# A selective scan on one core: every fourth state's output product moved from VectorE to GpSimd

## The chip, the core and the metric

The kernel runs on one core of a Trainium2 chip, as one launch that computes eight layers of a network on 3125 nodes. The metric is device time in microseconds. The change lies in one stage of the third layer, the selective scan.

## The reference, cut to what matters

The scan is the middle of `_mamba`. It runs along the 3125 nodes (in a sorted order) for 256 channels, each with 16 states.

```python
# dt, xc, z: [3125, 256]; Bm, Cm: [3125, 16]
A = -jnp.exp(A_log)                                # [256, 16]
dA = jnp.exp(dt[:, :, None] * A)                   # decay of each channel and state
dBx = (dt * xc)[:, :, None] * Bm[:, None, :]       # what each node drives into the state
def step(h, t):
    dA_t, dBx_t, C_t = t
    h = dA_t * h + dBx_t
    return (h, h @ C_t)                            # sum over the 16 states of h * C
_, y = lax.scan(step, jnp.zeros((256, 16)), (dA, dBx, Cm))
y = y + xc * D_param
y = y * jax.nn.silu(z)
return y @ out_proj_w.T
```

So for each state there is a recurrence along the nodes, and its result is multiplied by that state's row of `Cm` and summed over the states.

## The kernel before

`selective_scan` holds the channels on partitions (two halves of 128) and the nodes along the free dimension. The nodes are cut into 7 cuts of up to 447 (`CUTS`; the last has 443). Steps run over cut by cut and, inside a cut, over the 16 states: 112 steps, n = 16 x cut + state. In one step both halves lie side by side, 894 columns.

For step n the engines do this:

- SP loads the state's two rows, of B and of C, from `k.bc_d` in HBM and broadcasts them over all 128 partitions into `rows`, buffer n mod 4 (L2879). Before it reuses a buffer it waits until the drive (`ins_done`) and ScalarE's copy (`c_done`) of step n-4 are done (L2876, L2877). At state 4 of a cut it also loads `xc` and `z` for that cut.
- GpSimd makes the drive: row of B times `u` into `dB`, which has 3 buffers (L2899). It waits for the loaded row and for the scan of step n-3. From the second cut on it adds the carry of the cut before to the first column (L2904). At states 11 and 15 it also scatters one or two finished tiles each of the cut before with indirect DMAs (`move`, L2891).
- ScalarE makes the decays `dA` in PSUM, 2 buffers (L2945, L2946), two steps ahead; reads the carry out of `hh` (L2978); and copies the row of C into `row_c`, a single buffer in PSUM (L2956), when the product before is done.
- VectorE runs the recurrence over the 894 columns as one instruction, `dA` and `dB` into `hh`, 2 buffers (L3005), and then the product `pr` = `row_c` x `hh`, 2 buffers (L3013). Its order is scan n+1, product n. After a cut it adds `xc` x `dp` and multiplies by `z` (`finish`, L3020 and L3023), between the second scan and the first product of the next cut.
- TensorE adds each `pr` into `ps_y` by a multiplication with the identity (L2931), and projects the finished tiles of the cut before at states 4 and 9.

The order of the work on each engine is written out by hand; semaphores tie the engines together. GpSimd cannot read `row_c`, which is in PSUM; `rows` is in SBUF.

Of the kernel before, what the change touches and what calls it, by code (L numbers as in the profile page):

```python
# [8 lines left out]
ALU = mybir.AluOpType  # L9
# [2826 lines left out]
def selective_scan(k, z, dt, u, a_log, d_param, w_out, table):  # L2836


    nc = k.nc
    SN, CH, R = STATES, 447, 4  # L2840
# [2 lines left out]
    PROJECT_AT, KEEP_AT, MOVE_AT = (4, 9), (6, 11), (11, 15)  # L2843
    done_by = [0] + [hi // P for _, hi in CUTS]
    pair_of = lambda c, e: [t for t in range(done_by[c], done_by[c + 1]) if (t - done_by[c]) // 2 == e]
    moved_before = lambda n: sum(len(pair_of(q // 2, q % 2)) for q in range(n) if q % 2 == n % 2)
    with stage(k) as s:
        al, A, dp = s.sb("al", [128, 2, SN]), s.sb("A", [128, 2, SN]), s.sb("dp", [128, 2])
# [4 lines left out]
        xc = s.sb("xc", [128, 2, 2, CH])  # L2853
        dA, row_c, ps_y, ps_p = s.ps("dA", [128, 2, 1024]), s.ps("row_c", [128, 512]), s.ps("ps_y", [128, 2, 512]), s.ps("ps_p", [P, 2, D])
        gated, p_mm, p_read, moved = s.sem("gated"), s.sem("p_mm"), s.sem("p_read"), [s.sem(f"moved{e}") for e in range(2)]
        loaded, raised, negated, exps, carried, mixed, ins_done, c_done, scanned, prods, y_mm, y_read = (
            s.sem(n) for n in ("loaded", "raised", "negated", "exps", "carried", "mixed", "ins", "c_done", "scanned", "prods", "y_mm", "y_read"))
        cut_off, faded = s.sem("cut_off"), s.sem("faded")
        row_in = [s.sem(f"row_in{b}") for b in range(R)]
        pair_in = [s.sem(f"pair_in{c}") for c in range(len(CUTS))]  # L2860
# [6 lines left out]
        with s.block() as block:  # L2867
            @block.sync
            def _(sp):
                sp.dma_start(al[:], a_log.rearrange("(c p) n -> p c n", p=128)).then_inc(loaded, 16)  # L2870
                with nc.allow_non_contiguous_dma(reason="one number a channel"):
                    sp.dma_start(dp[:], d_param.rearrange("(c p) -> p c", p=128)).then_inc(loaded, 16)
                sp.dma_start(w_sb[:], w_out.rearrange("(c p) f -> p c f", p=128)).then_inc(loaded, 16)
                for n in range(STEPS):
                    if n >= R:
                        sp.wait_ge(ins_done, n - R + 1)  # L2876
                        sp.wait_ge(c_done, n - R + 1)  # L2877
                    lo, hi = cut(n)
                    sp.dma_start(rows[:, n % R, :, 0:hi - lo], k.bc_d[:, n % SN, lo:hi].partition_broadcast(128)).then_inc(row_in[n % R], 16)  # L2879
                    if n % SN == R:  # L2880
                        if n // SN >= 2:
                            sp.wait_ge(gated, n // SN - 1)
                        sp.dma_start(xc[:, n // SN % 2, :, 0:hi - lo], k.xc_d[:, :, lo:hi].rearrange("c p n -> p c n")).then_inc(pair_in[n // SN], 16)
                        sp.dma_start(z[:, :, lo:hi], k.z_d[:, :, lo:hi].rearrange("c p n -> p c n")).then_inc(pair_in[n // SN], 16)

            @block.gpsimd
            def _(pool):
                def move(c, e):
                    pool.wait_ge(p_read, 2 * c + e + 1)
                    for i, t in enumerate(pair_of(c, e)):  # L2890
                        nc.gpsimd.indirect_dma_start(table, bass.IndirectOffsetOnAxis(k.order_i[:, t:t + 1], 0), kept[:, e, i, :], None).then_inc(moved[e], 16)  # L2891

                for n in range(STEPS):
                    lo, hi = cut(n)
                    pool.wait_ge(row_in[n % R], 16 * (n // R + 1))
                    if n >= 3:
                        pool.wait_ge(scanned, n - 2)
                    into = halves(dB[:, n % 3, :], hi - lo)
                    ins = nc.gpsimd.tensor_tensor(into, both(rows[:, n % R, 0, 0:hi - lo], hi - lo), u[:, :, lo:hi], ALU.mult)  # L2899
                    if n >= SN:  # L2900
                        ins.then_inc(mixed, 1)
                        pool.wait_ge(mixed, n - SN + 1)
                        pool.wait_ge(carried, n - SN + 1)
                        ins = nc.gpsimd.tensor_tensor(into[:, :, 0:1], into[:, :, 0:1], carry[:, n % SN, :].unsqueeze(2), ALU.add)  # L2904
                    ins.then_inc(ins_done, 1)
                    if n >= SN and n % SN in MOVE_AT:
                        move(n // SN - 1, MOVE_AT.index(n % SN))
                for e in range(2):
                    move(len(CUTS) - 1, e)
                for e in range(2):  # L2910
                    pool.wait_ge(moved[e], 16 * moved_before(2 * len(CUTS) + e))

            @block.tensor
            def _(pe):
                def products(c, e):
                    pe.wait_ge(gated, c + 1)
                    if c or e:
                        pe.wait_ge(p_read, 2 * c + e)
                    for i, t in enumerate(pair_of(c, e)):
                        nc.tensor.matmul(ps_p[:, i, :], z[:, 0, t * P:(t + 1) * P], w_sb[:, 0, :], start=True, stop=False)  # L2920
                        ins = nc.tensor.matmul(ps_p[:, i, :], z[:, 1, t * P:(t + 1) * P], w_sb[:, 1, :], start=False, stop=True)
                    ins.then_inc(p_mm, 1)

                pe.wait_ge(loaded, 48)
                for n in range(STEPS):
                    st, c = n % SN, n // SN
                    pe.wait_ge(prods, n + 1)
                    if st == 0 and c:
                        pe.wait_ge(y_read, c)
                    for h in range(2):  # L2930
                        ins = nc.tensor.matmul(ps_y[:, h, 0:size(n)], k.ident[:], pr[:, n % 2, h * size(n):(h + 1) * size(n)], start=st == 0, stop=st == SN - 1)  # L2931
                    ins.then_inc(y_mm, 1)
                    if c and st in PROJECT_AT:
                        products(c - 1, PROJECT_AT.index(st))
                for e in range(2):
                    products(len(CUTS) - 1, e)

            @block.scalar
            def _(act):
# [12 lines left out]
                    ins.then_inc(faded, 1)  # L2952

                def outputs(n):
                    act.wait_ge(row_in[n % R], 16 * (n // R + 1))
                    nc.scalar.activation(row_c[:, 0:size(n)], rows[:, n % R, 1, 0:size(n)], ACT.Copy).then_inc(c_done, 1)  # L2956

# [14 lines left out]
                for n in range(STEPS):  # L2972
                    act.wait_ge(scanned, n + 1)
                    if n < LAST:
                        c, m = n // SN + 1, size(n)
                        act.wait_ge(faded, c)
                        for h in range(2):
                            ins = nc.scalar.activation(carry[:, n % SN, h:h + 1], hh[:, n % 2, (h + 1) * m - 1:(h + 1) * m], ACT.Copy, scale=fade[:, c, h, n % SN:n % SN + 1])  # L2978
                        ins.then_inc(carried, 1)
                        if n % SN == 2 and c + 1 < len(CUTS):  # L2980
                            fades(c + 1)
                    if n + 2 < STEPS:
                        decays(n + 2)
                    if n + 1 < STEPS:
                        act.wait_ge(prods, n + 1)
                        outputs(n + 1)
                    if n >= SN and n % SN in KEEP_AT:
                        keep(n // SN - 1, KEEP_AT.index(n % SN))
# [4 lines left out]
            def _(dve):  # L2993
# [3 lines left out]
                def scan(n):  # L2997
                    m = size(n)
                    dve.wait_ge(exps, n + 1)
                    dve.wait_ge(ins_done, n + 1)  # L3000
                    dve.wait_ge(cut_off, cleared(n))
                    if n >= 2:
                        dve.wait_ge(carried, min(n - 1, LAST))
                        dve.wait_ge(prods, n - 1)
                    nc.vector.tensor_tensor_scan(hh[:, n % 2, 0:2 * m], dA[:, n % 2, 0:2 * m], dB[:, n % 3, 0:2 * m], 0.0, ALU.mult, ALU.add).then_inc(scanned, 1)  # L3005

                def product(n):
                    m = size(n)
                    dve.wait_ge(c_done, n + 1)
                    if n >= 2:  # L3010
                        dve.wait_ge(y_mm, n - 1)
                    dve.wait_ge(scanned, n + 1)
                    nc.vector.tensor_tensor(halves(pr[:, n % 2, :], m), both(row_c[:, 0:m], m), halves(hh[:, n % 2, :], m), ALU.mult).then_inc(prods, 1)  # L3013
# [12 lines left out]
                for n in range(STEPS):  # L3026
                    if n + 1 < STEPS:
                        scan(n + 1)
                    if n % SN == 0 and n:
                        finish(n // SN - 1)  # L3030
                    product(n)
                finish(len(CUTS) - 1)


# [531 lines left out]
```

## Time and profile before

| what | us |
|---|---|
| median of 3 runs | 5497.91 (5497.24 to 5504.42) |
| the profiled execution, whole | 5502.4 |
| its span, first to last instruction | 5500.7 |
| the scan: first drive starts, last multiplication by `z` starts | 2212.32, 2583.39 |

Times in the rows below are microseconds from the span's start, mean durations in groups are in ns. An engine's idle time before an instruction stands in brackets with what ended it. DVE is VectorE, ACT is ScalarE, POOL is GpSimd, PE is TensorE, SP is the queue that issues most DMAs.

### The profile page before, as it was taken

What the parts mean: (1) busy time and instruction counts of PE and PEld (TensorE: products, weight loads), DVE (VectorE), ACT (ScalarE), POOL (GpSimd) and SP (SyncE); (2) the same over time, 40 slices, a digit from 0 to 9 for tenths busy, and PEclk for the clock granted to TensorE, in tenths of its full rate; (3) what the DMA queues carried; (4) which work ended last, traced back from release to release, by engine and by line L of the source; (5) the groups of instructions that cost most, each with busy time, mean ns of one, the idle gap of its engine ahead of it and who ended that gap; (6) DMA issues with size and microseconds to landing.
All of it is one profiled execution on the core that took longest, in us unless ns stands there. A gap on an engine that the chain in (4) does not pass through costs nothing. (4 is left out here: it accounts for less than half of the span.)

```text
span 5500.7 us, 66487 instructions
## 1 busy us (share of the span) xinstructions
PE 3947.6 (72%) x17366; PEld 2870.5 (52%) x17366; DVE 3294.1 (60%) x7107; ACT 2809.9 (51%) x6263; POOL 3077.3 (56%) x3130
## 2 busy tenths in 40 slices
PE   7999665659847888565386876878884964666766
PEld 4666444448735555222264446755654863333466
DVE  7555566656566777897746873266665126555543
ACT  5888433323346777564444543356662214777533
POOL 3777677724547776675304753447772233777334
PEclk8999878759968888898696997978785986777888
DMA  5555633356644444554203324644444314766357
GB/s 143 174 172 174 124 105 105 105 130 210 177 117 121 121 117 96 162 164 137 49 1 73 60 37 154 192 113 112 112 112 103 102 53 146 210 211 209 70 169 235
DMA packets 432744, 711.40 MB, mean 129 GB/s; under 512 B 150260, under 2 KB 312711, under 8 KB 427850
## 3 DMA queue, kind: packets, MB, share of 16 engines
q1 hardware_dynamic: 289247, 364.54, 23.5%
q0 software_dynamic: 139600, 337.72, 22.9%
q10 hardware_dynamic: 3530, 4.89, 0.3%
q8 instruction: 152, 2.49, 0.2%
q14 instruction: 215, 1.76, 0.1%
HBM read 559.31 MB, written 150.53 MB: 129 GB/s over the span
## 5 line engine op out<-in xcount | busy, mean ns | idle before, releaser
L631 PE MATMUL ps<-msg,same 128*125 128x256 f32 (+1 forms) x2496 | 947.6, 534 | 524.8 <-DMA msg<-rel_rows,src_rel 225.6
L631 PEld LDWEIGHTS ps<-msg,same 128*125 128x125 f32 x2496 | 580.6, 254 | 817.7 <-DVE msg L764 268.5
L607 POOL DMA_INDIRECT msg<-d_lin,src_i x416 | 393.7, 946 | 195.9 <-issue 94.2
L253 POOL DMA_INDIRECT rec<-rec,slot_i x391 | 380.4, 973 | 214.8 <-issue 93.5
L888 POOL DMA_INDIRECT msg<-d_gat,src_i x416 | 404.9, 973 | 134.4 <-issue 91.2
L607 POOL DMA_INDIRECT msg<-rel_rows,src_rel x416 | 398.0, 957 | 137.7 <-issue 83.2
L607 POOL DMA_INDIRECT msg<-d_gat,src_i x416 | 393.9, 947 | 133.6 <-issue 95.1
L2032 ACT ACTIVATE hid<-ps_h,w 128x128 f32<-128x128 f32 x572 | 210.1, 368 | 320.3 <-PE ps_h L1983 294.7
L278 PE MATMUL ps_f<-w,hs 128*128 128x256 f32 x1568 | 366.5, 387 | 8.4 <-DVE hs L422 8.0
L278 PEld LDWEIGHTS ps_f<-w,hs 128*128 128x128 f32 x1568 | 292.6, 191 | 105.3 <-issue 50.4
L949 PE MATMUL ps<-msg,same 128*125 128x260 f32 x832 | 278.8, 471 | 86.8 <-DVE agg_c L1111 86.5
L2931 PE MATMUL ps_y<-pr,ident 128*128 128x447 f32 (+1 forms) x448 | 211.3, 599 | 152.2 <-DVE pr L3013 152.2
L775 DVE TENSOR_TENSOR x<-x,ps 125x256 f32 x416 | 175.2, 421 | 217.1 <-PE ps L631 190.9
L1983 PE MATMUL ps_h<-xT,w 128*128 128x128 f32 x2288 | 294.1, 281 | 12.2 <-DMA w<-in_L_ffn_packed 11.6
L1983 PEld LDWEIGHTS ps_h<-xT,w 128*128 128x128 f32 x2288 | 284.6, 197 | 24.8 <-DMA w<-in_L_ffn_packed 15.9
L3089 POOL DMA_INDIRECT msg<-d_small,idx x256 | 242.4, 947 | 77.9 <-issue 77.9
L2899 POOL TENSOR_TENSOR dB<-rows,u 128x894 f32<-128x894 f32 (+1 forms) x112 | 215.2, 1923 | 117.2 <-DMA rows<-bc_d 85.7
L2070 DVE TENSOR_TENSOR y<-ps_o,b 128x256 f32<-128x256 f32 (+1 forms) x202 | 85.8, 425 | 314.4 <-PE ps_o L2008 243.6
L2058 DVE COPY xT<-ps_t 128x256 f32<-128x256 f32 (+1 forms) x186 | 83.0, 446 | 308.0 <-PE ps_t L1969 305.3
L422 DVE SCALAR_TENSOR_TENSOR hs<-ps_h,minus_b,hid 128x512 f32<-128x512 f32 x196 | 146.7, 749 | 195.6 <-ACT hid L357 194.9
L703 ACT ACTIVATE off<-ramp_r,minus_lo 128x125 f32<-128x125 f32 x832 | 260.4, 384 | 2.4 <-PEq L58 2.4
L3106 PE MATMUL ps<-spread,oh_lo 128*125 128x500 f32 x512 | 225.5, 594 | 40.1 <-DVE spread L3198 40.1
(626 smaller groups left out, 9921.0 us busy)
## 6 DMA issues: line engine op xcount, KB each, us to landing
w<-in_L_ffn_packed SPq DMA_DIRECT2D x170, 514.0 KB
fil<-rec SPq DMA_DIRECT2D x104, 512.0 KB, 4.2
rows<-bc_d SPq DMA_DIRECT2D x96, 447.0 KB
rel_rows<-row SPq DMA_DIRECT2D x25, 896.0 KB
got<-answered SPq DMA_DIRECT2D x30, 560.0 KB
ahead<-in_L_ffn_packed SPq DMA_DIRECT2D x8, 2052.0 KB
lo_rows<-ffn_lo_r SPq DMA_DIRECT2D x32, 500.0 KB
msg<-d_gat,src_i POOLq DMA_INDIRECT x832
```

What stands on the lines that cost most here:

```text
L253: nc.gpsimd.indirect_dma_start(k.rec, bass.IndirectOffsetOnAxis(slot_i[0:some_rows, c:c + 1], 0), rec[0:some_rows, g % R, j, :], None).the ...
L278: ins = nc.tensor.matmul(ps_f[:, v % 2, i, :], hs[:, (2 * g + c) % 4, j * 128:(j + 1) * 128], w2[:, c, :], start=c == 0, stop=c == 1)
L607: nc.gpsimd.indirect_dma_start(msg[:, g % R, j, :], None, table, bass.IndirectOffsetOnAxis(idx[:, n:n + 1], 0)).then_inc(msg_in[g % R], 16)
L631: nc.tensor.matmul(ps[:, j, 0:width], same[:, g % 2, j, :], msg[:, g % R, j, 0:width], start=True, stop=True).then_inc(mm, 1)
L703: ins = nc.scalar.activation(off[:, b, j, :], k.ramp_r1[:], ACT.Abs, bias=k.minus_lo1[:, n:n + 1])
L888: nc.gpsimd.indirect_dma_start(msg[:, g % R, j, :], None, table, bass.IndirectOffsetOnAxis(idx[:, n:n + 1], 0)).then_inc(msg_in[g % R], 16)
L949: nc.tensor.matmul(ps[:, n % 3, 0:width], same[:, g % 2, j, :], msg[:, g % R, j, 0:width], start=True, stop=True).then_inc(mm, 1)
L1983: ins = nc.tensor.matmul(ps_h[:, at % 4, 0:BR], part(n, c * x.f + f * 128, 128), xT[:, n % 2, c, :], start=c == 0, stop=c == 1)
L2899: ins = nc.gpsimd.tensor_tensor(into, both(rows[:, n % R, 0, 0:hi - lo], hi - lo), u[:, :, lo:hi], ALU.mult)
L2931: ins = nc.tensor.matmul(ps_y[:, h, 0:size(n)], k.ident[:], pr[:, n % 2, h * size(n):(h + 1) * size(n)], start=st == 0, stop=st == SN - 1)
L3089: nc.gpsimd.indirect_dma_start(msg[:, g % R, j, :], None, table, bass.IndirectOffsetOnAxis(idx[:, n:n + 1], 0)).then_inc(msg_in[g % R], 16)
L3106: nc.tensor.matmul(ps[:, 0:NT * W], oh_lo[:, g % 2, j, :], spread[:, g % 2, j, :], start=False, stop=False).then_inc(mm, 1)
```

## The change

States 3, 7, 11 and 15 of every cut (`on_pool`, 28 of the 112 steps) have their product made by GpSimd, which reads the row of C straight from `rows`. ScalarE makes no copy for these steps. In GpSimd's order the product of step n stands behind the drive of step n+2 and before a `move` of that step. SP frees those steps' row buffer by the new semaphore `pool_prods` instead of `c_done`. TensorE and VectorE's scans wait for both kinds of product; the counts of `prods` and `c_done` now count VectorE's steps alone. ScalarE's wait for the product before, ahead of a row copy, moves into `outputs` and is left out where there is no copy.

```diff
+    on_pool = lambda n: n % SN % 4 == 3
+    by_pool = lambda n: sum(1 for q in range(n + 1) if on_pool(q))
+    by_dve = lambda n: n + 1 - by_pool(n)
...
                     if n >= R:
                         sp.wait_ge(ins_done, n - R + 1)
-                        sp.wait_ge(c_done, n - R + 1)
+                        if on_pool(n - R):
+                            sp.wait_ge(pool_prods, by_pool(n - R))
+                        else:
+                            sp.wait_ge(c_done, by_dve(n - R))
...
+                def product(n):
+                    m = size(n)
+                    pool.wait_ge(scanned, n + 1)
+                    if n >= 2:
+                        pool.wait_ge(y_mm, n - 1)
+                    nc.gpsimd.tensor_tensor(halves(pr[:, n % 2, :], m), both(rows[:, n % R, 1, 0:m], m), halves(hh[:, n % 2, :], m), ALU.mult).then_inc(pool_prods, 1)
...
                     ins.then_inc(ins_done, 1)
+                    if n >= 2 and on_pool(n - 2):
+                        product(n - 2)
                     if n >= SN and n % SN in MOVE_AT:
                         move(n // SN - 1, MOVE_AT.index(n % SN))
+                for n in (STEPS - 2, STEPS - 1):
+                    if on_pool(n):
+                        product(n)
...
-                    pe.wait_ge(prods, n + 1)
+                    pe.wait_ge(prods, by_dve(n))
+                    if by_pool(n):
+                        pe.wait_ge(pool_prods, by_pool(n))
...
                 def outputs(n):
+                    if on_pool(n):
+                        return
+                    if n:
+                        act.wait_ge(prods, by_dve(n - 1))
...
-                        act.wait_ge(prods, n + 1)
                         outputs(n + 1)
...
-                        dve.wait_ge(prods, n - 1)
+                        dve.wait_ge(prods, by_dve(n - 2))
+                        if by_pool(n - 2):
+                            dve.wait_ge(pool_prods, by_pool(n - 2))
...
-                    dve.wait_ge(c_done, n + 1)
+                    dve.wait_ge(c_done, by_dve(n))
...
-                    product(n)
+                    if not on_pool(n):
+                        product(n)
```

## Rows read from the trace of the kernel before

**Rows 1.** Busy time by engine in a stretch: length, engines, PEclk, DMA share, GB/s.
```profile
2290.00:2370.00 80.00, 50.53 (x120) 21.85 (x120) 76.66 (x53) 52.52 (x131) 59.72 (x56) 0.96 0.55 165
```

**Rows 2.** Groups of instructions by line, of the scan's stretch, shapes apart.
```profile
L3005 DVE TENSOR_TENSOR_SCAN hh<-dA,dB 128x894 f32<-128x894 f32 x96 | 193.8, 2019 | 17.8 <-POOL dB L2899 5.3
L2899 POOL TENSOR_TENSOR dB<-rows,u 128x894 f32<-128x894 f32 x96 | 184.6, 1925 | 105.3 <-DMA rows<-bc_d 73.9 <-issue 28.3 <-ACT carry L2978 2.8
...
L3013 DVE TENSOR_TENSOR pr<-row_c,hh 128x894 f32<-128x894 f32 x96 | 102.1, 1064 | 0.0
...
L2956 ACT ACTIVATE row_c<-rows 128x447 f32<-128x447 f32 x96 | 52.5, 547 | 111.4 <-DVE pr L3013 111.4
...
L2904 POOL TENSOR_TENSOR dB<-dB,carry 128x2 f32<-128x2 f32 x96 | 21.5, 224 | 7.5
```

**Rows 3.** Waits in the scan's stretch: us in total, times, longest.
```profile
POOL dB L2899 <- DMA rows<-bc_d: 85.7, 78, 3.3
...
SPq L2877 <- ACT row_c L2956: 302.5, 108, 4.4
```

**Rows 4.** Timeline of VectorE: start, length, instruction; a state, and a cut's end.
```profile
2300.26 2.02 DVE L3005 TENSOR_TENSOR_SCAN hh<-dA,dB 128x894 f32<-128x894 f32 x1
2302.20 1.06 DVE L3013 TENSOR_TENSOR pr<-row_c,hh 128x894 f32<-128x894 f32 x1
2303.39 2.02 DVE L3005 TENSOR_TENSOR_SCAN hh<-dA,dB 128x894 f32<-128x894 f32 x1
...
2319.05 2.02 DVE L3005 TENSOR_TENSOR_SCAN hh<-dA,dB 128x894 f32<-128x894 f32 x1
...
2322.26 1.09 DVE L3023 TENSOR_TENSOR z<-xc,z 128x894 f32<-128x894 f32 x1
2323.27 1.08 DVE L3013 TENSOR_TENSOR pr<-row_c,hh 128x894 f32<-128x894 f32 x1
```

**Rows 5.** Timeline: a row buffer's last reader, and the drive on its next row.
```profile
2222.40 0.55 ACT L2956 ACTIVATE row_c<-rows 128x447 f32<-128x447 f32 x1 [1.10 <-DVE pr L3013]
...
2226.89 1.93 POOL L2899 TENSOR_TENSOR dB<-rows,u 128x894 f32<-128x894 f32 x1 [0.89 <-DMA rows<-bc_d]
...
2290.77 0.55 ACT L2956 ACTIVATE row_c<-rows 128x447 f32<-128x447 f32 x1 [1.10 <-DVE pr L3013]
...
2294.76 1.77 POOL L2899 TENSOR_TENSOR dB<-rows,u 128x894 f32<-128x894 f32 x1 [0.39 <-DMA rows<-bc_d]
...
2303.29 0.55 ACT L2956 ACTIVATE row_c<-rows 128x447 f32<-128x447 f32 x1 [1.10 <-DVE pr L3013]
...
2308.61 1.77 POOL L2899 TENSOR_TENSOR dB<-rows,u 128x894 f32<-128x894 f32 x1 [0.48 <-DMA rows<-bc_d]
```

**Rows 6.** Timeline of GpSimd: the first drives, and one pass over two scatter DMAs.
```profile
2212.32 9.43 POOL L2899 TENSOR_TENSOR dB<-rows,u 128x894 f32<-128x894 f32 x5 [28.26 <-issue]
2224.08 1.92 POOL L2899 TENSOR_TENSOR dB<-rows,u 128x894 f32<-128x894 f32 x1 [2.33 <-DMA rows<-bc_d]
...
2349.60 1.23 POOL L2891 DMA_INDIRECT d_sorted<-kept,order_i  x1 [0.18 <-issue]
2351.13 1.19 POOL L2891 DMA_INDIRECT d_sorted<-kept,order_i  x1 [0.30 <-issue]
2352.34 1.94 POOL L2899 TENSOR_TENSOR dB<-rows,u 128x894 f32<-128x894 f32 x1
...
2354.50 1.93 POOL L2899 TENSOR_TENSOR dB<-rows,u 128x894 f32<-128x894 f32 x1
```

**Rows 7.** Timeline of VectorE and GpSimd at a cut's end; the last product.
```profile
2325.11 1.92 POOL L2899 TENSOR_TENSOR dB<-rows,u 128x894 f32<-128x894 f32 x1 [2.76 <-DMA rows<-bc_d]
...
2374.68 1.39 DVE L3023 TENSOR_TENSOR z<-xc,z 128x894 f32<-128x894 f32 x1
2375.20 0.92 POOL L2904 TENSOR_TENSOR dB<-dB,carry 128x2 f32<-128x2 f32 x1
...
2579.16 1.08 DVE L3013 TENSOR_TENSOR pr<-row_c,hh 128x886 f32<-128x886 f32 x1 [0.66 <-ACT row_c L2956]
```

More of the change, by code:

```diff
@@ L2855, in selective_scan @@
         gated, p_mm, p_read, moved = s.sem("gated"), s.sem("p_mm"), s.sem("p_read"), [s.sem(f"moved{e}") for e in range(2)]
-        loaded, raised, negated, exps, carried, mixed, ins_done, c_done, scanned, prods, y_mm, y_read = (
-            s.sem(n) for n in ("loaded", "raised", "negated", "exps", "carried", "mixed", "ins", "c_done", "scanned", "prods", "y_mm", "y_read"))
+        loaded, raised, negated, exps, carried, mixed, ins_done, c_done, scanned, prods, pool_prods, y_mm, y_read = (
+            s.sem(n) for n in ("loaded", "raised", "negated", "exps", "carried", "mixed", "ins", "c_done", "scanned", "prods", "pool_prods", "y_mm", "y_read"))
         cut_off, faded = s.sem("cut_off"), s.sem("faded")
```

## The prediction

> **What bounds the kernel now.** The edit touches one stage, so I read first the busy time of each engine in a stretch in the middle of it. In 80 us VectorE works 76.66 us; GpSimd works 59.72, ScalarE 52.52, TensorE 50.53, at a clock granted at 0.96 (the 2.4 GHz level for nearly all of it) and with the DMA engines busy for a share of 0.55 [rows 1]. VectorE sets the pace. The groups of instructions then say with what: 112 scans (`hh`) of about 2.02 us and 112 products (`pr`) of 1.06; GpSimd has 112 drives (`dB`, the first factor times a loaded row) of about 1.92, and 96 carry additions of 0.22 [rows 2]. The list of waits shows what stands close behind VectorE: GpSimd stood 78 times, 85.7 us in all, for a row that had not yet landed, and SP's queue stood 302.5 us for ScalarE's copy to give a row buffer back [rows 3]. So rows are fetched as late as their four buffers allow. Last comes the timeline, which gives the pitches. A scan starts 1.94 us before the product behind it, and that product 1.19 us before the next scan: 3.13 us a state [rows 4]. Sixteen states and the cut's end (scan at 2319.05 to next product at 2323.27, 4.22, less the usual 1.94: 2.3; 0.3 more where a drive stands beside the multiplication by `z` [rows 4, 7]) make 52.4 to 52.7 us a cut.
>
> **What the change takes away.** 28 of the 112 products leave VectorE. Each frees 1.19 us of its line, less about 0.1 for the start of the scan that now follows a scan directly: four states cost VectorE 4 x 3.13 - 1.1 = 11.4 us in place of 12.5. If VectorE stayed the bound this were 28 x 1.1 = 31 us. 28 row copies of 0.55 us leave ScalarE, which is no bound [rows 1, 2]: worth nothing by themselves.
>
> **What it adds.** 28 products on GpSimd. The trace has none, but the drive has the same shape, operand kinds and broadcast: 1.93 in the mean, 1.77 to 1.94 in single rows [rows 2, 5, 6]; VectorE's 1.06 bounds it from below, and from above I allow 2.8, a drive held up once as the carry addition of 0.92 was [rows 7]. The ends are worth 24 us each way over 28 products; I take 1.93, the row of the same form. That work fits: sixteen drives with carries at a pitch of 2.16 (2352.34 to 2354.50), four products, and four scatter DMAs at 1.46 each (2349.42, where the first one's wait begins, to 2352.34 for two) are 34.6 + 7.7 + 5.8 = 48.1 us a cut [rows 6], under the 52.7 of today and level with VectorE's 48.3.
>
> **What it moves: who gives the fourth row buffer back.** States 3, 7, 11, 15 all lie in buffer 3 of `rows`. Today the copy on ScalarE frees it. From that copy's end to the start of the drive on the row loaded into its place, where that drive waited for it, I read 3.44 us (2291.32 to 2294.76) at the best, 3.94 (2222.95 to 2226.89) in a quiet stretch of the first cut, and 4.77 (2303.84 to 2308.61) behind scatter DMAs [rows 5]. The loads in question will start away from the scatters, so I take the middle one, L = 3.9. After the change GpSimd's own product frees the buffer, and GpSimd needs the new row four states on. In its program order state n's product stands behind the drive of n+2, so from the end of one product to the end of the next there is: L, in which only the drive of n+3 has room; then the drives of n+4, n+5, n+6 in a row; then the product. That is a closed loop, on an engine that looks three quarters busy:
>
> - plain: 3.9 + 3 x 2.15 + 1.93 = 12.3, against VectorE's 11.4 and today's 12.5;
> - with the scatter DMAs, which stand behind the drives of states 11 and 15, that is between the drive of n+4 and that of n+5, and so inside the loop and never under L: 1.46 more for each tile, 15.2 for two;
> - at a cut's end the loop goes through VectorE. The scan of state 17 waits for the product of 15 because it writes the same `hh` buffer; then come the cut's end, the product of 16, ScalarE's copy of row 17, the load of row 21 and its drive, and only then the product of 19: 2.0 + 2.4 + 1.1 + 0.65 + 3.9 + 2.15 + 1.93 = 14.2;
> - in the first cut, with no carries or scatters (five drives in 9.43 us, 1.88 each [rows 6]): 3.9 + 5.6 + 1.93 = 11.5, and 12.0 for the third, into the next cut.
>
> **The sum.** From the product of state 3 to that of state 111 there are 27 periods: first cut 11.5 + 11.5 + 12.0 = 35.0; six cut ends 6 x 14.2 = 85.2; six plain ones 73.8; eleven with scatters 11 x 12.3 + 19 tiles x 1.46 = 163.0; the last has no drives behind it, 3.9 + 2.15 + 2.92 + 1.93 = 10.9. Together 367.9 us. The first starts from the drive at 2224.08, which ends at 2226.00; the product of state 3 stands behind it and ends at 2227.9 [rows 6]. The last would end at 2595.8; today's last product starts at 2579.16 and ends at 2580.24 [rows 7]. That is 15.5 us later, and the cut end, the last projections and the barrier follow as today. By cuts: the first gains about 4, each later one loses 3 to 4, the last gets some back. The profiled execution took 5502.4 us, of which the span is 5500.7; the sum makes it 5518. It lies 4.5 above the median of the runs, 5497.91, on which I put the forecast: 5513 us.
>
> **Contention between VectorE and GpSimd.** The row: multiplying `z` by `xc`, both in SBUF, VectorE takes 1.09 us at 2322.26, where GpSimd stands idle until its drive at 2325.11, and 1.39 at 2374.68 beside a drive, when GpSimd's little carry addition took 0.92 instead of 0.19 [rows 4, 7]. Scan and product hold 2.02 and 1.06 throughout [rows 2]: they read one input from PSUM. So I charge the new products nothing for their neighbours. The Trainium skill, "Perfetto Trace Analysis", section "Optimizing Scalar/DVE Operations", warns that the two engines share a read port and that moving work between them might not help; "SBUF — State Buffer", section "Who interferes with whom", narrows it to VectorE instructions with two SBUF inputs. By the first, taken for every pair, each product could hold a scan for its 1.93 us, 54 us more in all; by the second, and by this trace, 0.
>
> **Rivals.**
>
> A, the load is quick: the row for buffer 3 is now asked for in a quiet moment and lands at the shortest L seen, 3.44. 27 x 0.46 = 12.4 us come back, the loss is 3 us: 5501. For it: DMA engines busy for 0.55 only [rows 1]. Against: SP finds the next buffer already free and issues that row right behind, so two loads share the engines.
>
> B, the load is slow: those two in flight, and the scatters beside them, give the longest, 4.77: 27 x 0.87 = 23 us more, 5536. A product of 2.3 us instead of 1.93 would give 10 of these.
>
> C, faster: the buffer loop does not close and VectorE sets the pace at 11.4. It decides where L + 6.45 + 1.93 is under 11.4, at L below 3.0, and needs the scatters off the loop as well. 31 us less: 5467. For it: the first cut, where I expect a gain too, and GpSimd's work by itself, which fits. Against: no row in buffer terms is under 3.44, and two in four periods have a scatter.
>
> **Chances.** The forecast (5509 to 5531) 0.57; A (5487 to 5509) 0.23; B (over 5531) 0.10; C (under 5487) 0.10. A difference under 0.2%, 11 us, cannot be told from none here. So slower 0.67, same 0.23, faster 0.10. The range 5497 to 5534 leaves out C, the lower edge of A, and most of B.
>
> **What would show it.** Right: VectorE's idle time in the stage grows from next to nothing to some 40 us, and it waits for GpSimd's product (`pr`, or the scan behind it) and for `dB`; GpSimd's waits for the rows from DMA fall at every fourth drive, right before the drive of states 7, 11, 15 of a cut, 1 to 2 us each; ends of its products lie 12.3 us apart in plain periods, near 15 with a scatter, and 11.5 in the first cut; SP waits for GpSimd's product at every fourth issue. The first cut shorter than today's 50 us, the others longer than 52.7. Wrong: VectorE still busy for over 90% of the stage (C); products on GpSimd well off 1.93 us; scans longer than 2.02 us beside them; or the distance from a product's end to the drive on its buffer's next row not near 3.9.

## The result, and the profile after

The changed kernel takes 5529.32 us (median of 4 runs, 5523.0 to 5535.81) beside 5497.57 for the kernel before (4 runs): a ratio of 1.0055, interval 1.0042 to 1.0068, 23 to 37 us slower. The forecast was slower, 5513, in a range of 5497 to 5534.

The profiled executions differ by 24.1 us in span, somewhat less than the medians, and all of it is in the scan: from its first scan instruction to the first VectorE instruction of the next stage there are 384.6 us before (2214.33 to 2598.91) and 409.5 after (2224.08 to 2633.62).

Busy time by engine in a stretch of the stage after, columns as in [rows 1]:

```profile
2310.00:2390.00 80.00, 49.71 (x103) 20.43 (x101) 61.88 (x41) 41.40 (x105) 64.20 (x57) 0.84 0.48 144
```

VectorE fell from 76.66 of 80 us [rows 1] to 61.88. GpSimd, with a quarter of the products added, is busy for 64.20 only, and TensorE's granted clock fell from 0.96 to 0.84. No engine is full: a sign of a loop. The groups of instructions, beside [rows 2]:

```profile
L3030 DVE TENSOR_TENSOR_SCAN hh<-dA,dB 128x894 f32<-128x894 f32 x96 | 193.5, 2019 | 59.0 <-POOL pr L2904 22.3 <-POOL dB L2917 18.1 <-DVE pr L3038 12.4
L2912 POOL TENSOR_TENSOR dB<-rows,u 128x894 f32<-128x894 f32 x96 | 186.2, 1943 | 87.1 <-DMA rows<-bc_d 48.0 <-issue 27.8 <-ACT carry L3002 10.9
...
L3038 DVE TENSOR_TENSOR pr<-row_c,hh 128x894 f32<-128x894 f32 x72 | 76.6, 1064 | 0.0
...
L2904 POOL TENSOR_TENSOR pr<-rows,hh 128x894 f32<-128x894 f32 x24 | 46.0, 1917 | 0.0
```

Scan and product kept their lengths, 2019 and 1064 ns. GpSimd's product takes 1917 ns, the drive's price. The idle time before the scans grew from 17.8 to 59.0 us, and GpSimd's product and drive ended most of it. Waits in the stage after, beside [rows 3]:

```profile
POOL dB L2912 <- DMA rows<-bc_d: 58.5, 30, 3.2
...
DVE hh L3030 <- POOL pr L2904: 26.6, 21, 2.2
DVE hh L3030 <- POOL dB L2917: 20.6, 19, 2.3
...
SPq L2881 <- POOL pr L2904: 160.0, 27, 8.7
```

GpSimd now waits for rows 30 times in place of 78, once or so in each of the 27 periods between its products, 2 us each. SP's queue waits 27 times for GpSimd's product. Here is one such loop in GpSimd's timeline after, from one product to the next with two scatter DMAs between them, columns as in [rows 6]:

```profile
2353.53 1.91 POOL L2904 TENSOR_TENSOR pr<-rows,hh 128x894 f32<-128x894 f32 x1
2355.40 1.92 POOL L2912 TENSOR_TENSOR dB<-rows,u 128x894 f32<-128x894 f32 x1
...
2359.53 1.92 POOL L2912 TENSOR_TENSOR dB<-rows,u 128x894 f32<-128x894 f32 x1 [1.93 <-DMA rows<-bc_d]
2361.53 0.19 POOL L2917 TENSOR_TENSOR dB<-dB,carry 128x2 f32<-128x2 f32 x1
2361.90 1.22 POOL L2897 DMA_INDIRECT d_sorted<-kept,order_i  x1 [0.18 <-issue]
2363.42 1.19 POOL L2897 DMA_INDIRECT d_sorted<-kept,order_i  x1 [0.30 <-issue]
2364.63 1.94 POOL L2912 TENSOR_TENSOR dB<-rows,u 128x894 f32<-128x894 f32 x1
...
2366.80 1.92 POOL L2912 TENSOR_TENSOR dB<-rows,u 128x894 f32<-128x894 f32 x1
...
2368.94 1.91 POOL L2904 TENSOR_TENSOR pr<-rows,hh 128x894 f32<-128x894 f32 x1
```

The product ends at 2355.44. One drive runs under the load, then GpSimd stands 1.93 us until the row is in, 4.09 after the product. Two scatters and two drives follow, and the next product ends at 2370.85: 15.41 us, where 15.2 was predicted. VectorE in the same stretch:

```profile
2348.27 1.06 DVE L3038 TENSOR_TENSOR pr<-row_c,hh 128x894 f32<-128x894 f32 x1
2349.56 2.02 DVE L3030 TENSOR_TENSOR_SCAN hh<-dA,dB 128x894 f32<-128x894 f32 x1 [0.23 <-DVE pr L3038]
...
2366.93 2.02 DVE L3030 TENSOR_TENSOR_SCAN hh<-dA,dB 128x894 f32<-128x894 f32 x1 [1.90 <-POOL dB L2917]
2370.98 2.02 DVE L3030 TENSOR_TENSOR_SCAN hh<-dA,dB 128x894 f32<-128x894 f32 x1 [2.03 <-POOL pr L2904]
```

It stands 1.90 us for the drive behind the scatters and 2.03 for GpSimd's product. The first two lines show something else: a scan behind VectorE's own product starts 1.29 us after the product's start, against 1.19 [rows 4]. It has one semaphore more to wait for.

### The profile page after: what moved, and what is told of

Read it like the earlier page. It is cut to its first block and busy times, and to the rows that moved or that the text cites. A ratio compares the mean times of both kernels' runs of the same rounds, so it can differ in the third digit from the quotient of the medians.

```text
span 5524.8 us, 66642 instructions
## 1 busy us (share of the span) xinstructions
PE 3966.9 (72%) x17366; PEld 2869.4 (52%) x17366; DVE 3269.5 (59%) x7079; ACT 2796.1 (51%) x6235; POOL 3126.5 (57%) x3158
## 5 line engine op out<-in xcount | busy, mean ns | idle before, releaser
L2951 PE MATMUL ps_y<-pr,ident 128*128 128x447 f32 (+1 forms) x448 | 229.6, 644 | 160.3 <-DVE pr L3038 108.7
L3030 DVE TENSOR_TENSOR_SCAN hh<-dA,dB 128x894 f32<-128x894 f32 (+1 forms) x112 | 225.5, 2016 | 67.9 <-POOL pr L2904 26.6
```

## The experiments

All ran in interleaved rounds with the kernel before; the ratio is to it, with its 95% interval, and 0.0010 of it is 5.5 us. Gains and losses below are worked out from the ratios.

| version | median us | ratio (interval) |
|---|---|---|
| 1: changed, 8 row buffers | 5494.76 | 0.9975 (0.9966 to 0.9985) |
| 2: before, 8 row buffers | 5505.87 | 0.9997 (0.9988 to 1.0006) |
| 3: changed, scatters behind states 10 and 14 | 5509.51 | 1.0010 (1.0001 to 1.0018) |
| 4: before, extra work on GpSimd | 5504.13 | 0.9995 (0.9987 to 1.0004) |
| 5: changed, 8 row buffers, one wait | 5481.60 | 0.9962 (0.9949 to 0.9975) |
| 6: changed, one wait | 5534.66 | 1.0060 (1.0047 to 1.0073) |
| 7: four products, all buffers, one wait | 5466.67 | 0.9944 (0.9928 to 0.9961) |
| 8: changed, 5 row buffers | 5491.27 | 0.9979 (0.9969 to 0.9990) |
| 9: version 7 with no product on GpSimd | 5474.70 | 0.9959 (0.9946 to 0.9973) |
| 10: changed, products at 3, 7, 11 only | 5523.33 | 1.0044 (1.0031 to 1.0058) |
| 11: before, three `hh` buffers | 5487.64 | 0.9972 (0.9961 to 0.9984) |
| 12: version 7 with three products | 5458.22 | 0.9923 (0.9909 to 0.9936) |

Beside versions 1 to 4 the kernel before took 5507.2 us, beside 5 to 8 5501.58, beside 9 and 10 5498.33, beside 11 and 12 5502.77.

**1, 2 and 8: is it the loop through the fourth buffer?**

```diff
-    SN, CH, R = STATES, 447, 4
+    SN, CH, R = STATES, 447, 8        # version 8: 5; version 2: 8, in the kernel before
```

> The changed kernel with 8 row buffers in place of 4, nothing else. Theory A (the buffer loop: a GpSimd product gives back the buffer whose next row GpSimd itself needs four states on): the loop now spans eight states and no longer decides, so the loss goes and the gain appears, about 17 us faster than the kernel before (5480), 47 us faster than the changed kernel; not the full 31, since the scan two states on still waits for the product (one hh buffer of two) and the cut's end waits for the product of state 15. GpSimd's wait for rows from DMA falls from 58 us to under 15. Rival B (GpSimd's product is simply too slow at 1.92 us against VectorE's 1.06, or the two hold each other up at SBUF): buffers change nothing, it stays about 30 us slower than before.

> The kernel before with 8 row buffers: the control for the run with 8 buffers in the changed kernel. Theory A: no change, within 3 us of before, since VectorE sets the pace at 3.13 us a state and the rows already come in time; GpSimd's 86 us of waiting for rows turns into waiting for the scan. If this one is faster too, a part of what 8 buffers give has nothing to do with who releases them. Rival B expects no change either.

> The changed kernel with one row buffer more, 5 in place of 4. Theory A: what costs is that the product of state n releases the buffer for n+4, with three drives and the next product still to come behind that load; one buffer more moves the wait behind the drive of n+4 and breaks the loop. So it gives nearly all that 8 buffers gave: 10 to 17 us faster than before, 40 to 47 faster than the changed kernel. Rival (8 buffers helped by having the rows early, whatever the loop): a fifth buffer is a quarter of that step, so it would stay between, at or above the time of before.

Only the buffers differ, and the loss of 30 us turned into a gain of 12 to 14, with 5 as with 8; the kernel before did not care. So the rival, that the loss comes from a GpSimd product that is too slow or contends, falls. With 8 buffers GpSimd never stands for rows for a time worth a line. In a period with scatters it works without a stop from one product to the next, 13.67 us. Its waits in the stage are now small ones for the scan and for TensorE:

```profile
POOL dB L2912 <- DVE hh L3030: 11.3, 8, 3.3
...
POOL pr L2904 <- PE ps_y L2951: 9.3, 5, 2.5
```

The two products at the ends of that period in GpSimd's timeline of version 1:

```profile
2294.88 1.92 POOL L2904 TENSOR_TENSOR pr<-rows,hh 128x894 f32<-128x894 f32 x1 [0.94 <-DVE hh L3030]
...
2308.55 1.92 POOL L2904 TENSOR_TENSOR pr<-rows,hh 128x894 f32<-128x894 f32 x1
```

The gain was 3 us smaller than the 17 expected; version 5 finds more than that in the second wait.

**3: are the scatters inside the loop?**

```diff
-    PROJECT_AT, KEEP_AT, MOVE_AT = (4, 9), (6, 11), (11, 15)
+    PROJECT_AT, KEEP_AT, MOVE_AT = (4, 9), (6, 11), (10, 14)
```

> The changed kernel with the scatter DMAs behind the drives of states 10 and 14 instead of 11 and 15, four row buffers as it was. Theory A: at 10 and 14 they stand between the product and the drive that waits for the released buffer, that is under the time of the load and off the loop, where they cost at most what the load leaves over. By the same sum 17 to 21 us faster than the changed kernel, about 5510, still slower than before by some 10. Of the 27 periods from product to product none should be over 15 us, except cut ends. Rival B: GpSimd has the same work, so no change against the changed kernel.

It is 25 us faster than the changed kernel (1.0055 to 1.0010), a little more than the 17 to 21 expected, and 18 faster in the profiled stage. Rival B falls. GpSimd's timeline in version 3: the scatters stand where the load is on its way, and the period is 13.45 us. That is GpSimd's own work, 4 x 2.15 + 1.92 + 2.92, and no longer the load's.

```profile
2347.76 1.92 POOL L2904 TENSOR_TENSOR pr<-rows,hh 128x894 f32<-128x894 f32 x1
...
2352.00 1.22 POOL L2897 DMA_INDIRECT d_sorted<-kept,order_i  x1 [0.18 <-issue]
...
2354.75 1.93 POOL L2912 TENSOR_TENSOR dB<-rows,u 128x894 f32<-128x894 f32 x1
...
2361.21 1.91 POOL L2904 TENSOR_TENSOR pr<-rows,hh 128x894 f32<-128x894 f32 x1
```

**4: does GpSimd's load cost by itself?** In the kernel before:

```diff
                     ins.then_inc(ins_done, 1)
+                    if n >= 2 and (n - 2) % SN % 4 == 3:
+                        pool.wait_ge(scanned, n - 1)
+                        nc.gpsimd.tensor_tensor(halves(spare, hi - lo), both(u[:, 0, lo:hi], hi - lo), u[:, :, lo:hi], ALU.mult)
```

> The kernel before, with an extra GpSimd multiplication of 128x894 from SBUF (u times u into a spare tile that nobody reads) at exactly the 28 places where the change puts its products, after the same wait for the scan; VectorE still makes all products and ScalarE's copies still release all row buffers. It gives GpSimd the change's load without the release. Theory A: within 4 us of before; VectorE's scans stay at 2.02 us and its products at 1.06. Rival B: if GpSimd's load or the shared reading of SBUF is what costs, 10 to 30 us slower, with longer scans or products, or VectorE waiting for the drives.

No change. In the groups of version 4 the scans beside it keep 2019 ns; the extra instruction took 1723 ns, so it is a little lighter than the product.

```profile
L3008 DVE TENSOR_TENSOR_SCAN hh<-dA,dB 128x894 f32<-128x894 f32 x96 | 193.8, 2019 | 18.0 <-POOL dB L2899 5.5 <-POOL dB L2904 0.4
...
L2908 POOL TENSOR_TENSOR spare<-u 128x894 f32<-128x894 f32 x23 | 39.6, 1723 | 0.0
```

**5 and 6: the second wait on VectorE.** TensorE likewise:

```diff
-                        dve.wait_ge(prods, by_dve(n - 2))
-                        if by_pool(n - 2):
+                        if on_pool(n - 2):
                             dve.wait_ge(pool_prods, by_pool(n - 2))
+                        else:
+                            dve.wait_ge(prods, by_dve(n - 2))
```

> The changed kernel, four row buffers, in which each scan on VectorE waits for one kind of product only (GpSimd's or its own, whichever used that hh buffer), and TensorE the same. In the changed kernel's trace the scan behind a product starts 0.23 us after it in place of 0.13. Theory A: in the loop VectorE has idle time in most periods, so 0.1 us on some 80 scans hardly counts; it counts where the loop passes through VectorE, six cut ends and the first cut: 0 to 3 us faster than the changed kernel. Rival (the second wait on VectorE is a part of the loss by itself): 84 x 0.1 = 8 us faster than the changed kernel.

> Eight row buffers in the changed kernel and one kind of product to wait for at each scan and at TensorE. With 8 buffers alone it was 14 us faster than before. Theory A: VectorE sets the pace again in the periods without scatters, so the 0.1 us now counts there: 4 to 8 us faster than with 8 buffers alone, 18 to 22 us faster than before (5475 to 5480 beside 5498 before). Rival (GpSimd's own work sets the pace in every period): no change against 8 buffers alone.

With four row buffers it gave nothing (1.0060 beside 1.0055), although the pitch from product to scan did fall back to 1.19 us, as VectorE's timeline of version 6 shows; the loop ate it. With 8 it gave some 7 us more (0.9975 to 0.9962; the intervals overlap, but the profiled stage is 6 us shorter too), as expected. The same edit is worth nothing or 7 us, depending on what bounds.

```profile
2343.42 1.06 DVE L3040 TENSOR_TENSOR pr<-row_c,hh 128x894 f32<-128x894 f32 x1
2344.61 2.02 DVE L3032 TENSOR_TENSOR_SCAN hh<-dA,dB 128x894 f32<-128x894 f32 x1
```

**7, 9, 11 and 12: a version that beats both, and why.** Version 7 has six row buffers, four of `dB`, three of `hh` and `pr`, one wait, each GpSimd product issued behind the drive three states on, and:

```diff
-    on_pool = lambda n: n % SN % 4 == 3
+    on_pool = lambda n: n % SN in (2, 5, 8, 12)   # 9: False; 12: in (1, 4, 10)
```

> A version meant to be fast: GpSimd's products at states 2, 5, 8, 12 instead of 3, 7, 11, 15 (none at a cut's end, and apart from the scatters behind the drives of 11 and 15), issued one drive later, six row buffers, four of dB, three of hh and of pr, and one kind of product to wait for. Theory A: no loop through GpSimd is longer than VectorE's line, so nearly the whole 28 x 1.1 = 31 us appear: 26 to 31 us faster than before. If GpSimd's load itself set the pace, it would stay near the version with eight row buffers, 14 to 20 us faster.

It gave 31 us, the expected number, but the control shows that the reason was mostly another:

> Control for the fastest version: the same buffers (six of rows, four of dB, three of hh and pr) and waits, but no product on GpSimd: VectorE makes all 112 and ScalarE copies all rows. Theory A: VectorE paces the scan at 3.13 us a state as before, so within 3 us of before; what made the fast version fast is then GpSimd's share of the products and not the buffers. If the buffers alone help, it is 5 us or more faster than before.

With no product on GpSimd at all the buffers alone gave 22 us. My theory had them at 0: a miss, and the 31 of version 7 came out by luck. What its four products a cut add to the buffers is some 8 us, with intervals that overlap. VectorE's timeline in version 9 has a pitch of 2.91 us (3.13 in [rows 4]):

```profile
2300.86 2.00 DVE L3032 TENSOR_TENSOR_SCAN hh<-dA,dB 128x894 f32<-128x894 f32 x1
2302.79 1.05 DVE L3040 TENSOR_TENSOR pr<-row_c,hh 128x894 f32<-128x894 f32 x1
2303.77 2.00 DVE L3032 TENSOR_TENSOR_SCAN hh<-dA,dB 128x894 f32<-128x894 f32 x1
```

Version 11 gives the kernel before a third `hh` buffer and nothing else:

```diff
-                    if n >= 2:
-                        dve.wait_ge(carried, min(n - 1, LAST))
-                        dve.wait_ge(prods, n - 1)
+                    if n >= 3:
+                        dve.wait_ge(carried, min(n - 2, LAST))
+                        dve.wait_ge(prods, n - 2)
```

> The kernel before with a third hh buffer, nothing else. In the control for the fastest version, without products on GpSimd, a state took VectorE 2.91 us (scan to scan) in place of 3.13, with no idle time. Theory C: in the kernel before each scan waits for the completion of the product issued right before it, since that product read the hh buffer that the scan writes; a third buffer makes it wait for the product of a state earlier, long done, and the 0.22 us at each of 112 states go: 20 to 25 us faster than before. Rival (it was the third pr buffer or the fourth dB buffer): no change.

15 us faster (9 to 22), with the pitch at 2.91 in its trace as well: most of the 22, and less than I expected. In the kernel before each scan waits for the completion of the product issued right before it on the same engine, and 0.22 us a state go between them. The third buffer also loosens the scan's wait for ScalarE's reading of the carry (`carried`). In the last cut no carry is read, and the pitch is 3.11 us before and 2.89 in version 11, the same 0.22 less, so it is the product's wait that costs. The lines are VectorE's, of the kernel before and, below them, of version 11:

```profile
2569.31 2.00 DVE L3005 TENSOR_TENSOR_SCAN hh<-dA,dB 128x886 f32<-128x886 f32 x1
...
2572.42 2.00 DVE L3005 TENSOR_TENSOR_SCAN hh<-dA,dB 128x886 f32<-128x886 f32 x1
```

```profile
2543.71 1.98 DVE L3005 TENSOR_TENSOR_SCAN hh<-dA,dB 128x886 f32<-128x886 f32 x1
...
2546.60 1.98 DVE L3005 TENSOR_TENSOR_SCAN hh<-dA,dB 128x886 f32<-128x886 f32 x1
```

What of the rest belongs to `dB`, `pr` and `rows` was not taken apart.

> The fastest version with three products a cut on GpSimd (states 1, 4, 10) in place of four. Theory: with four, GpSimd is the bound (busy 76.4 of 80 us, 47 to 49 us a cut), and VectorE idles; a product less takes 1.93 us a cut from GpSimd and gives VectorE 1.0 back, so that both have 45 to 46.5 us a cut: 5 to 14 us faster than with four, 36 to 45 faster than before. If GpSimd is not the bound, it is 7 us slower than with four.

Three products a cut are 42 us faster than before, the fastest version run and as expected; 20 of the 42 are more than the buffers alone gave (version 9), with intervals that don't overlap. Busy time in 80 us of version 7 and, below it, version 12:

```profile
2290.00:2370.00 80.00, 54.97 (x126) 24.30 (x124) 75.08 (x53) 51.90 (x133) 76.40 (x67) 0.91 0.63 187
```

```profile
2290.00:2370.00 80.00, 54.91 (x130) 24.62 (x131) 79.93 (x56) 54.41 (x139) 75.24 (x66) 0.94 0.61 185
```

With four GpSimd is the fuller engine and VectorE waits (75.08); with three VectorE has no idle time left in this stretch (79.93). The states were moved as well, so number and place of the products were not told apart.

**10: the cut's end.** `on_pool = lambda n: n % SN in (3, 7, 11)` in the changed kernel.

> The changed kernel with GpSimd's products at states 3, 7 and 11 alone; state 15 goes back to VectorE, four row buffers. In the trace of the changed kernel six periods over a cut's end last 15.2 us in the mean, against the 14.2 of the prediction: TensorE's last accumulation waits for the product of state 15, comes at the 1.2 GHz level of the clock in some cuts (3.2 us in place of 1.8), and the multiplication by z stretches beside a drive. If that is where the prediction was short, taking state 15 away gives 8 to 13 us back against the changed kernel, though it takes a quarter of the relief from VectorE: about 5518 to 5523 beside 5498 before. If the cut's end is not what was mis-sized, only the sum's own 4 us come back.

1.0044 beside 1.0055: about 6 us by the ratios, with intervals that overlap. The 8 to 13 us did not come, and the sum's own 4 us would explain most of it. It doesn't settle what the cut's end costs; the trace of the changed kernel says more, below.

## Why the prediction was right, and where it was short

**The loop.** Right. Product to product on GpSimd, by its 28 products in the trace after, the first and the last of which are

```profile
2235.26 1.92 POOL L2904 TENSOR_TENSOR pr<-rows,hh 128x894 f32<-128x894 f32 x1
...
2614.55 1.91 POOL L2904 TENSOR_TENSOR pr<-rows,hh 128x886 f32<-128x886 f32 x1
```

| periods | predicted us | measured us |
|---|---|---|
| first cut, 3 | 35.0 | 35.5 |
| over a cut's end, 6 | 85.2 | 91.2 |
| plain, 6 | 73.8 | 74.9 |
| with scatters, 11 | 163.0 | 166.9 |
| last | 10.9 | 10.7 |
| together | 367.9 | 379.3 |

The first product ends 13.1 us after the first scan's start, the last 392.4; before, the last product ended at 365.9 (2580.24 less 2214.33). So the trace's loss up to the last product is 26.5 us, the predicted 15.5 and the 11.4 by which the periods were short, less 0.4; some 2 us come back behind it, which leaves the 24.1 of the spans. The median of the runs lies 16 us above the 5513 of the forecast. The periods account for 11 of them, of which those 2 came back. The other 7 or 8 are no part of the trace: the medians lie 32 us apart and the two profiled executions 24, both inside the interval of 23 to 37.

**The terms that were too small.** L, put at 3.9, was 4.2 in the mean over the 27 loads (3.69 to 5.08). In the 21 periods without a cut's end it was 4.18: 0.28 more each, 5.9 us, and those periods were 5.3 short. That is the term of the sum that was mis-sized there. Rival B had the direction right, a slower load, with 0.87 more. Why the loads were slower is not shown. Six us lie at the cut's ends, put at 14.2 us (its terms add up to 14.1) and 14.4 to 16.3 long. One of the two longest looks like this in the timeline of the trace after:

```profile
2504.44 3.22 PE L2951 MATMUL ps_y<-pr,ident 128*128 128x447 f32 x4 [4.38 <-POOL pr L2904]
...
2507.70 1.27 DVE L3045 SCALAR_TENSOR_TENSOR xc<-xc,dp,ps_y 128x447 f32<-128x447 f32 x2 [1.25 <-PE ps_y L2951]
2508.48 1.77 POOL L2912 TENSOR_TENSOR dB<-rows,u 128x894 f32<-128x894 f32 x1 [1.88 <-DMA rows<-bc_d]
2509.01 2.19 DVE L3048 TENSOR_TENSOR z<-xc,z 128x894 f32<-128x894 f32 x1
```

And busy time there, the granted clock third from the end, with the window before it below:

```profile
2504.00:2508.00 4.00, 3.22 (x4) 1.18 (x4) 2.32 (x2) 0.14 (x1) 2.52 (x3) 0.57 0.63 149
2498.00:2502.00 4.00, 1.77 (x4) 0.68 (x4) 1.72 (x2) 1.33 (x3) 3.90 (x4) 1.00 0.35 98
```

TensorE stood 4.38 us for GpSimd's product, its granted clock fell to 0.57 (mostly the 1.2 GHz level, where the window before has 1.00), and its accumulation took 3.22 us in place of 1.77. The cut's end waits for it, 1.25 us. Then the multiplication by `z`, both inputs in SBUF, began beside a drive: 2.19 us against 1.09 [rows 4]. The drive ended at 2510.25, 1.24 us after that beginning, and 0.95 are left, about what the multiplication takes alone: as if it had stood until then. In another cut the multiplication began first, by 0.01 us, and the drive stretched, to 2.86 us in place of 1.92:

```profile
2450.02 1.09 DVE L3048 TENSOR_TENSOR z<-xc,z 128x894 f32<-128x894 f32 x1
```

```profile
2450.03 2.86 POOL L2912 TENSOR_TENSOR dB<-rows,u 128x894 f32<-128x894 f32 x1 [2.35 <-DMA rows<-bc_d]
```

The Trainium skill, "SBUF — State Buffer", section "Who interferes with whom", says that a VectorE instruction with two SBUF inputs contends with a GpSimd instruction that reads SBUF, and that the lock on their shared ports is exclusive; both rows agree. Over the six cut ends VectorE stood 0, 0, 0.51, 1.04, 1.25 and 1.26 us for an accumulation that took 1.74 to 3.22 us, and `z` was stretched by 1.1 and 1.0 in the last two. Together that is 6.2 us, against the 6.0 that were missing. The prediction had no term for the slower accumulation. The stretch of `z` it had read as 0.3 us [rows 7], and its 2.4 for the cut's end holds next to nothing for it.

**The price of the product** (1.93, measured 1.92) and the untouched scans came out. The first cut was shorter, by 2.4 us to the next cut's first scan and 3.3 to its second, where about 4 had been said. That VectorE's idle time would grow came out, and by more than the 40 us: from the first scan to the end of the last multiplication by `z` it was 17 us before (370.14 less 352.83 busy) and 71 after (396.91 less 326.28).

**The relief.** 31 us was the ceiling named for the case that VectorE sets the pace. With the loop open (versions 1, 8 and 5) 12 to 21 came. What remains in version 1 are GpSimd's full periods with scatters, 7.9 us in which scans stood for its products, and 0.1 us for the second semaphore at each scan behind a product of VectorE's own. Version 5 takes that last one away. The prediction missed it: the section on the change named the wait, and the sum charged nothing for it.

## What to carry to other kernels

When work moves to an idle engine, ask what that engine gives back and what it needs next: if it releases the buffer whose refill it waits for itself, add up that loop, with everything that stands in its order between the two, before trusting its busy share. One buffer more opened the loop here. And run the control with the buffers alone: here half of the best version's gain, 22 of 42 us, came with the buffers alone, most of it from a wait that one more of them removed.

## What the runs showed that I had not expected

- A scan that waits for the completion of the product just issued on its own engine costs VectorE 0.22 us a state (3.13 to 2.91); the trace before books 0.13 of it as idle time, with no other engine to blame.
- A second semaphore to wait for, long since raised, delayed VectorE's scans by 0.1 us (1.19 to 1.29 from product to scan).
